# One handover of a transformer block on one core: the first feed-forward unit moved to other PSUM banks and one place ahead on TensorE

## The reference, cut to what matters

```python
# x: (16, 256, 256), cond_emb: (16, 256, 192), 16 heads of 64, D_FF = 1024, float32
h = _layernorm(x, ln1_g, ln1_b)
x = _attention(h, h, sa_wq, sa_wk, sa_wv, sa_wo, sa_bo) + x
h = _layernorm(x, ln2_g, ln2_b)
x = _attention(h, cond_emb, ca_wq, ca_wk, ca_wv, ca_wo, ca_bo) + x
h = _layernorm(x, ln3_g, ln3_b)
p = h @ ff_w1 + ff_b1
a, gate = (p[..., :D_FF], p[..., D_FF:])
h = a * jax.nn.gelu(gate, approximate=False) @ ff_w2 + ff_b2
return h + x
```

## Time and profile before

| | before |
|---|---|
| three runs, us | 1720.36, 1722.38, 1723.20 (median 1722.38) |
| profiled execution, us | 1720.33, span 1718.5 |
| TensorE busy | 1701.5 us, 99% of the span |
| VectorE, ScalarE, GpSimd busy | 86%, 69%, 63% |
| granted TensorE clock, mean | 0.999 |
| chain that ended last | TensorE 94%, VectorE 2%, others 1% or less each |

### The profile page before, as it was taken

The page is one execution under the profiler, slowest core; times in us unless marked ns, Lnnn a source line. Parts: engine busy times, 40 slices in busy tenths (PEclk is TensorE's granted clock), DMA queues, the critical chain, the costliest instruction groups (busy, mean ns, idle before and its releaser), DMA issues.

```text
span 1718.5 us, 42973 instructions
## 1 busy us (share of the span) xinstructions
PE 1701.5 (99%) x13628; PEld 1663.3 (97%) x13628; DVE 1470.9 (86%) x3188; ACT 1186.7 (69%) x3245; POOL 1082.9 (63%) x1808
## 2 busy tenths in 40 slices
PE   8999999999999999999999999999999998999999
PEld 7999999999999999999999999999999997888888
DVE  7888988988888888899999999999999987666665
ACT  6777777777777777777778878777777775222222
POOL 6877777766666666687778777777777664122211
PEclk9999999999999999999999999999999999999999
DMA  6877777676666566667778877776666662212210
GB/s 193 198 179 180 185 180 178 167 180 170 152 153 157 151 161 159 166 166 187 190 190 193 193 194 178 185 180 168 167 167 168 163 171 56 74 50 63 67 44 25
DMA packets 286641, 263.99 MB, mean 154 GB/s; under 512 B 102224, under 2 KB 246736, under 8 KB 286416
## 3 DMA queue, kind: packets, MB, share of 16 engines
q1 hardware_dynamic: 230992, 246.55, 56.9%
q10 hardware_dynamic: 55424, 14.70, 4.0%
HBM read 70.40 MB, written 24.90 MB: 55 GB/s over the span
## 4 chain that ended last, share of the span: by engine, by line
PE 94%; DVE 2%; ACT 1%; POOL 1%; DMA 1%; issue 1%; SPq 1%; ACTq 0%; POOLq 0%; DVEq 0%
PE QKB L341 19%; PE PVB L400 14%; PE PTB L355 12%; PE WOP L380 10%; PE VB L316 9%; PE S L303 7%; PE S L302 7%; PE S L898 5%; PE PTB L898 5%; PE QKB L914 3%; PE VB L914 3%; ACT PT L507 0%; DVE NM L610 0%; ACT PH L526 0%; DVE PL L592 0%
## 5 line engine op out<-in xcount | busy, mean ns | idle before, releaser
L507 ACT ACTIVATE PT<-S,NM 128x256 f32<-128x256 f32 x1024 | 472.1, 474 | 190.3 <-DVE NM L610 189.9
L592 DVE TENSOR_TENSOR PL<-PTB,PH 128x512 fp32r<-128x512 f32 x512 | 349.9, 684 | 85.9 <-ACT PH L526 79.9
L797 POOL TENSOR_TENSOR ON<-ON,RB 128x256 f32<-128x256 f32 x256 | 188.8, 738 | 283.0 <-DVE ON L624 268.6
L526 ACT ACTIVATE PH<-PTB 128x1024 fp32r<-128x1024 f32 x256 | 263.4, 1029 | 94.7 <-PE PTB L355 91.6
L610 DVE TENSOR_REDUCE NM<-S 128x2 f32<-128x512 f32 x512 | 326.1, 678 | 0.4 <-PE S L290 0.3
L355 PE MATMUL PTB<-IDN,PT 128*128 128x128 f32 x2048 | 267.4, 273 | 5.1 <-DVE PL L592 4.9
L302 PE MATMUL S<-RX 128*128 128x256 f32 x1012 | 253.7, 283 | 0.0
L303 PE MATMUL S<-RX 128*128 128x256 f32 x1012 | 253.7, 283 | 0.0
L355 PEld LDWEIGHTS PTB<-IDN,PT 128*128 128x128 f32 x2048 | 230.0, 140 | 7.0 <-DVE PL L592 6.6
L380 PE MATMUL WOP<-WO,OT 128*128 128x256 f32 x1536 | 226.3, 283 | 2.0 <-POOL OT L802 2.0
L624 DVE TENSOR_TENSOR ON<-PVB,ON 64x256 f32<-64x256 f32 x512 | 213.3, 417 | 3.5
(11 more groups left out here) (136 smaller groups left out, 3141.3 us busy)
## 6 DMA issues: line engine op xcount, KB each, us to landing
RX<-QKS SPq DMA_DIRECT2D x506, 192.0 KB, 2.9
RX<-QKS SPq DMA_DIRECT2D x506, 128.0 KB, 2.8
RB<-denominators SPq DMA_DIRECT2D x512, 64.0 KB, 2.6
out_dram<-XR SPq DMA_DIRECT2D x32, 256.0 KB, 2.7
rows<-XN SPq DMA_DIRECT2D x24, 256.0 KB, 2.5
rows<-HF SPq DMA_DIRECT2D x23, 256.0 KB, 2.5
XR<-in_x_dram SPq DMA_DIRECT2D x16, 256.0 KB, 3.1
denominators<-RDT SPq DMA_DIRECT2D x256, 16.0 KB
```

Source lines behind the costliest of these rows:

```text
L507: last = e.activation(PT[:, c % 2, j * S:(j + 1) * S], S1[:, i, qt * S:(qt + 1) * S], ACT.Exp, bias=NM[:, j:j + 1], accum_out=DEN[:, c % 2 ...
L526: e.activation(PH[:, s % 2, :], PTB[:, :, :].rearrange("p i n -> p (i n)"), ACT.Copy) \
L592: e.tensor_tensor(PL[:, cols], PTB[:, i, :], PH[:, s % 2, cols].bitcast(F32), ALU.subtract).then_inc(a.dve_pl, 1)
```

## The change

In the order of the diff:

- `act_slot`: the eight loads of chunk 0's rows are issued two a slot in slots 248 and 249 instead of one a slot in 248 to 251 (on SyncE the same). `act_ffn_h` runs for one half in slot 252 and for the other in 253, ahead of PH there, instead of both in 254. In slot 254, behind PH, the new `act_ffn_round_h` rounds both.
- `dve_slot`: the second half of PL is made right behind the first from slot 254 on; so slot 255 has no left-over half at its start.
- The rounded rows of chunk 0 (and of all even chunks) go to QKS instead of RX.
- Unit 0's F1 goes to the banks QKB and VB (`gates`); `AG` is swapped, so unit 1 goes to S1 and unit 2 to PTB. Unit 0 waits for the last evacuations of QKB and VB, unit 1 for the last exponentials, unit 2 for the last PL.
- `dve_ffn_turn` runs in slots 250 and 251 instead of 252 and 253. `dve_ffn_split` is gone: in slot 254 VectorE waits for the last odd ring copy and makes only the low parts (`dve_ffn_low`).
- In the hand-written loops the unit now comes first, then the slot, on TensorE, VectorE and ScalarE. GpSimd's order is as it was.

```diff
@@ -513,11 +513,10 @@
             elif sl.has(c + AHEAD) and not -1 <= c < DIRECT - 1:
                 act_copy_qk(e, c + AHEAD)
 
-            if ATT - 8 <= c < ATT - 4:
-                load_ffn_rows(e, 0, 2 * (c - ATT + 8) + 1)
-            if c == ATT - 2:
-                act_ffn_h(e, 0, 0)
-                act_ffn_h(e, 0, 1)
+            if ATT - 8 <= c < ATT - 6:
+                load_ffn_rows(e, 0, 4 * (c - ATT + 8) + 1, 4 * (c - ATT + 8) + 3)
+            if c in (ATT - 4, ATT - 3):
+                act_ffn_h(e, 0, c - ATT + 4)
 
             if sl.has(c - 1):
                 s = c - 1
@@ -525,6 +524,10 @@
                 sl.wait(e, a.pe_pv, s - 1)
                 e.activation(PH[:, s % 2, :], PTB[:, :, :].rearrange("p i n -> p (i n)"), ACT.Copy) \
                     .then_inc(a.act_ph, 1)
+
+            if c == ATT - 2:
+                act_ffn_round_h(e, 0)
+                act_ffn_round_h(e, 1)
 
             if prepares and pair == 1:
                 act_load_rows(e, seq + 1, *(range(2, 4) if seq else range(4)))
@@ -613,7 +616,7 @@
             if 0 < c < DIRECT:
                 dve_split_qk(e, c + 2)
 
-            if sl.has(c - 2):
+            if sl.has(c - 2) and c < ATT - 1:
                 dve_p_low(e, c - 2, 1)
 
             if sl.has(c - 3):
@@ -654,6 +657,8 @@
                 sl.wait(e, a.act_ph, c)
                 sl.wait(e, a.pe_pv, c - 1)
                 dve_p_low(e, c - 1, 0)
+                if c >= ATT - 2:
+                    dve_p_low(e, c - 1, 1)
 
             if pair == 3 and c > PAIRS:
                 n = seq - 1
@@ -834,8 +839,9 @@
 
         fs = FfnStages()
 
-        RXF = RX[:, :, :, :, :].rearrange("p r i u s -> p (r i u s)")
-        FHT = ((RXF[:, 0:KD * CW], RXF[:, KD * CW:2 * KD * CW]), (PH[:, 0, :], PH[:, 1, :]))
+        QKF = QKS[:, :, :, :].rearrange("p r u s -> p (r u s)")
+        FHT = ((QKF[:, 0:KD * CW], QKF[:, KD * CW:2 * KD * CW]), (PH[:, 0, :], PH[:, 1, :]))
+        RINGS = sum(k % 2 for k in range(DIRECT, ATT))
 
         def rounded(chunk, part, k):
 
@@ -845,8 +851,12 @@
             .rearrange("p (r a s) -> p r a s", r=2, a=2)
         FG = PT[:, 0, :].rearrange("p (r s) -> p r s", r=2)
         FV = PT[:, 1, :].rearrange("p (r s) -> p r s", r=2)
-        AG = (S1, PTB)
+        AG = (PTB, S1)
         OB = (QKB, VB)
+
+        def gates(c, g):
+
+            return (QKB, VB)[g][:, :] if c == 0 else AG[c % 2][:, g, :]
 
         ROWS = (XN[:, :], HF[:, :])
         TURNED = (STG[:, 0:CW], STG[:, CW:2 * CW])
@@ -884,8 +894,11 @@
                 sl.wait(e, fs.dve_hf, c - 1)
                 if c == 0:
                     e.wait_ge(s_pw, 2 * QTR * NCH)
+                    e.wait_ge(a.dve_lo, ATT)
+                    e.wait_ge(a.dve_vf, ATT)
+                if c == 1:
                     e.wait_ge(a.act_exp, 2 * ATT)
-                if c == 1:
+                if c == 2:
                     e.wait_ge(a.dve_pl, 2 * ATT)
                 if c == FU - 1:
                     pe_ffn_first(e, chunk, f, 0).then_inc(fs.pe_f1, 1)
@@ -895,7 +908,7 @@
                         n = 0
                         for k in range(KD):
                             for wp, ap in ((0, 0), (0, 1), (1, 0)):
-                                last = e.matmul(AG[c % 2][:, g, :], w1(k, wp, g * FF + f * P),
+                                last = e.matmul(gates(c, g), w1(k, wp, g * FF + f * P),
                                                 rounded(chunk, ap, k), start=n == 0, stop=n == 5)
                                 n += 1
                     last.then_inc(fs.pe_f1, 1)
@@ -940,6 +953,11 @@
             e.activation(ROWS[k], ROWS[k], ACT.Identity, bias=LNG[:, 2, 1, k:k + 1],
                          scale=LNG[:, 2, 0, k:k + 1]).then_inc(fs.act_hf, 1)
 
+        def act_ffn_round_h(e, k):
+
+            e.wait_ge(fs.act_hf, k + 1)
+            e.activation(rounded(0, 0, k), ROWS[k], ACT.Copy).then_inc(fs.s_hh, 1)
+
         def act_ffn(e, sl):
             c = sl.c
             if sl.has(c):
@@ -955,7 +973,7 @@
                     e.activation(FG[:, c % 2, S:CW], last_half(1)[:, S:CW], ACT.Gelu,
                                  bias=B1[:, PAIRS + f:PAIRS + f + 1]).then_inc(fs.act_g, 1)
                 else:
-                    e.activation(FG[:, c % 2, :], AG[c % 2][:, 1, :], ACT.Gelu,
+                    e.activation(FG[:, c % 2, :], gates(c, 1), ACT.Gelu,
                                  bias=B1[:, PAIRS + f:PAIRS + f + 1]).then_inc(fs.act_g, 1)
             if c >= 0 and c % PAIRS == 6 and sl.has(c + PAIRS):
                 for k in range(KD):
@@ -970,15 +988,11 @@
                                    TURNED[h].rearrange("p (b k t i) -> p k t b i", b=4, k=KD, t=TT)[:, k])
             last.then_inc(fs.dve_th, 1)
 
-        def dve_ffn_split(e, sl, chunk):
-            for k in range(KD):
-                sl.wait(e, fs.act_hf, KD * chunk + k + 1)
-                if k == 0:
-                    sl.wait(e, fs.pe_f1, PAIRS * (chunk - 1))
-                e.tensor_copy(rounded(chunk, 0, k), ROWS[k]).then_inc(fs.s_hh, 1)
-                sl.wait(e, fs.s_hh, KD * chunk + k + 1)
-                e.tensor_tensor(rounded(chunk, 1, k), ROWS[k], rounded(chunk, 0, k).bitcast(F32),
-                                ALU.subtract).then_inc(fs.s_ht, 1)
+        def dve_ffn_low(e, k):
+
+            e.wait_ge(fs.s_hh, k + 1)
+            e.tensor_tensor(rounded(0, 1, k), ROWS[k], rounded(0, 0, k).bitcast(F32),
+                            ALU.subtract).then_inc(fs.s_ht, 1)
 
         def pool_ffn_split(e, chunk):
             for k in range(KD):
@@ -1013,7 +1027,7 @@
             elif sl.has(c):
                 r = c % 2
                 sl.wait(e, fs.act_g, c + 1)
-                e.scalar_tensor_tensor(FV[:, r, :], AG[r][:, 0, :], B1[:, f:f + 1], FG[:, r, :],
+                e.scalar_tensor_tensor(FV[:, r, :], gates(c, 0), B1[:, f:f + 1], FG[:, r, :],
                                        ALU.add, ALU.mult).then_inc(fs.dve_hf, 1)
                 sl.wait(e, fs.dve_hf, c + 1)
                 sl.wait(e, fs.pe_f2, c - 1)
@@ -1112,10 +1126,12 @@
                 dve_normalize(e, zero_ffn, fs, 0, ROWS, (0, 1))
             if c == ATT - 10:
                 dve_normalize(e, zero_ffn, fs, 0, ROWS, (2, 3))
-            if ATT - 4 <= c < ATT - 2:
-                dve_ffn_turn(e, 0, c - ATT + 4)
-            if c == ATT - 1:
-                dve_ffn_split(e, zero_ffn, 0)
+            if ATT - 6 <= c < ATT - 4:
+                dve_ffn_turn(e, 0, c - ATT + 6)
+            if c == ATT - 2:
+                e.wait_ge(d_dup[1], 16 * COPIES * RINGS)
+                dve_ffn_low(e, 0)
+                dve_ffn_low(e, 1)
 
         def pool_low(e, *ns):
 
@@ -1292,8 +1308,8 @@
                     store_rows(c // PAIRS + 1)
                 if c in (ATT - 10, ATT - 9):
                     store_ffn_rows(0, c - ATT + 10)
-                if ATT - 8 <= c < ATT - 4:
-                    load_ffn_rows(e, 0, 2 * (c - ATT + 8))
+                if ATT - 8 <= c < ATT - 6:
+                    load_ffn_rows(e, 0, 4 * (c - ATT + 8), 4 * (c - ATT + 8) + 2)
                 if 1 <= c <= ATT:
                     save_den(c - 1)
                 if 0 <= c - 1 + AHEAD < ATT and c - 1 >= -AHEAD:
@@ -1351,8 +1367,8 @@
             act_weights(e, 4, 5)
             run_slots(-AHEAD, ATT + 1, ATT, lambda sl: act_attention_slot(e, sl))
             for j in range(2):
+                act_ffn(e, Slot(j, FU, 2))
                 act_slot(e, Slot(ATT + 1 + j, ATT))
-                act_ffn(e, Slot(j, FU, 2))
             ffn(e, act_ffn, 2)
 
         @block.vector
@@ -1375,8 +1391,8 @@
             dve_weights(e, 5)
             run_slots(-AHEAD, ATT + 1, ATT, lambda sl: dve_attention_slot(e, sl))
             for j in range(3):
+                dve_ffn(e, Slot(j, FU, 2))
                 dve_slot(e, Slot(ATT + 1 + j, ATT))
-                dve_ffn(e, Slot(j, FU, 2))
             e.wait_ge(a.dve_xo, 2 * B)
             ffn(e, dve_ffn, 3)
 
@@ -1390,8 +1406,8 @@
             e.wait_ge(s_ring, 4)
             run_slots(-AHEAD, ATT, ATT, lambda sl: pe_attention_slot(e, sl))
             for j in range(4):
+                pe_ffn(e, Slot(j, FU, 2))
                 pe_slot(e, Slot(ATT + j, ATT))
-                pe_ffn(e, Slot(j, FU, 2))
             ffn(e, pe_ffn, 4)
 
 
```

## The result

| | before | after |
|---|---|---|
| median of 13 runs each, us | 1721.35 (1719.46 to 1723.20) | 1725.75 (1723.35 to 1727.67) |
| ratio, 95% interval | | 1.0026 (1.0018 to 1.0033) |
| profiled execution: its time and span, us | 1720.33, 1718.5 | 1726.59, 1724.8 |

The change makes the kernel 4.4 us slower. To compare executions I measure one stretch on TensorE, from the start of PV(249) (slot 251, up to which the PV products start in the same rhythm before and after) to the start of F1(6) (where the rhythm is the same again), and call it **the handover**. It is 55.27 us before (1415.53 to 1470.80) and 60.49 us after (1416.65 to 1477.14): 5.2 us more.

The account below looks back on a forecast made before the run. TensorE bound nearly everywhere; at the handover, its loop with VectorE. Terms 0.63 + 0.17 - 0.33 + 0.18 - 3.0 + 1.7 + 2.2, about +1.5 us, took the profiled execution to 1721.8; forecast 1723.1, range 1719.2 to 1726.2.

Parts of the forecast that it names:

- the likeliest case: Whole kernel: a measured time within 0.2%, 3.4 us, of no change, chance 0.72; the forecast sum was about +1.5 us.
- the rival of the drain: At the table load before gelu(0): a real drain makes F2(0) 1.4 later; +2.9, about 1724.5 us; chance 0.06.
- the clock: Rival: gaps before PV(253) and F2(0) drop TensorE to 1.2 GHz; two falls, +4.7, about 1726.3 us; chance 0.08.
- the loop of TensorE and VectorE: From slot 253 on: NM, PL, ON, PV, PL hold TensorE; waits to F1(0) about 7.7 us, the most returnable.
- Parts 1 and 2: Slots 250 to 253: earlier loads and turns, +0.63; gain and bias a slot apart ahead of PH, +0.17 and -0.33.
- Part 3: Slots 254 and 255: P low in one turn and only low parts on VectorE put PV(253) later, +0.18 more.
- Part 4: Ahead of slot 256: F1(0) follows PV(253) without a wait, none before WO(252), T(255), PV(254); -3.0 us.
- First late unit: Before F2(0): gelu(0) stands behind PH(255) and the table load, so TensorE waits +1.7 us (1.3 to 2.4).
- Second late unit: Before F2(3): GpSimd's OT, bias adds and 1/sigma hang on the later WO(254); TensorE waits +2.2 us (0 to 2.9).

Follow-up runs that it names:

- e8_turn_early: The kernel before with only the earlier row loads and turns and the gain and bias steps in slots 252 and 253 ahead of PH: 1720.38 us.
- e6_gain_behind: e5 with ScalarE's gain and bias steps of slots 252 and 253 behind PH instead of ahead of it: 1719.23 us.
- e3_low_later: The changed kernel with VectorE's two low parts of chunk 0's rows moved from the end of slot 254 to behind ON(252) in slot 255: 1722.71 us.
- e9_table_early: e6_gain_behind with an unread one-column gelu on ScalarE in slot 256, between ON(253) and PH(255), to load the table early: 1717.99 us.
- e2: The changed kernel with GpSimd's 1/sigma for chunk 1 ahead of its four bias adds for chunk 0: 1722.70 us.
- e4: The changed kernel with the edits of e2 and e3_low_later together: 1720.76 us.
- e5: e4 with GpSimd's 1/sigma of chunk 1 moved once more, to ahead of OT(255), behind the product ON of slot 258: 1719.46 us.
- e1_fill: The changed kernel with unread identity transposes filling TensorE's gaps before PV(253), F2(0) and F2(3), every wait kept: 1722.54 us.
- e7_order_back: The changed kernel with the hand-written loops of TensorE, VectorE and ScalarE back to the slot first, then the unit: 1722.15 us.
- e10_pl_apart: The changed kernel with P low in two turns again, the second half at the start of the next slot: 1725.28 us.

## Why the prediction was right and wrong

The time lies in the range (1725.75 in 1719.2 to 1726.2), but the likeliest case was "within 0.2%, +1.5 us" and the measured is +4.4, just beyond it, where I had put 0.18. That it lies in the range is luck. The range's upper end came from the rival of the drain (1724.5 + 1.5, which is 1726.0, not the 1726.2 that I wrote; the lower end adds up to 1719.4, not 1719.2), and no drain showed. The forecast's own time, 1723.1, with the same 1.5 for the spread of runs would have ended at 1724.6, and the rival that came true, the clock, stood at 1726.3, outside. Point by point:

- **Bound by the loop of TensorE and VectorE; gaps, not busy time**: right. All that the experiments gained came from gaps and from the falls of the clock behind them.
- **Parts 1 and 2**, +0.63, +0.17, -0.33 (in sum +0.63, +0.80, +0.47 at PV(250), (251), (252)): measured +0.53, +0.66, +0.35 in after, and the same in e8_turn_early. ScalarE's steps ahead of PH were named as what ate the gain of the turn's removal; e6_gain_behind shows 1.06 us for it.
- **Part 3**, PV(253) at +0.65: measured 22.80 for 21.75, +1.05. The step that was too short is "the two low parts at 1434.6 and 1435.2", 0.61 each: the first took 1.21, and GpSimd's split of V ran at the same time (1435.50 to 1436.23). That these two stand on the path was in the sum, but as a term of a whole of +0.18 it was not seen as what it is, the largest thing to mend: e3_low_later gains 3 us by moving them, 1.6 of it the fall of the clock.
- **Part 4**, F1(0) behind PV(253) without a wait, and none before WO(252), T(255), PV(254): right.
- **First late unit**, +1.7: measured 1.50 idle, 1.65 by start times (1447.34 + 2.75 to 1451.74). The chain (T(255), PH(255), table load, gelu) is as written; e9_table_early takes the load out of it.
- **Second late unit**, +2.2: measured 2.20 idle, 2.36 by starts. e2, e4 and e5 show its cause; VectorE waited 5.28 for 1/sigma.
- **The clock**: this is what the forecast's sum left out. I had it as a rival at 0.08, two falls, +4.7 in all, priced 1.5 each; measured two falls, 1.6 each (e1_fill), +4.4. Its places were half right: behind the gap before PV(253), as written, but not behind the one before F2(0) (1.50), where the clock stayed at 1.00; the second fall came before F2(3), at the gap of 2.20 that the rival had not counted. The argument against it was that from 1430 to 1450 TensorE had been busy 15.6 of 20 us at 1.00. That stretch was too long a look: its gaps were 1.08, 0.85 and 1.32, each on its own:

```profile
1436.47 0.66 PE L355 MATMUL PTB<-IDN,PT 128*128 128x128 f32 x4 [1.08 <-DVE PL L592]
...
1442.05 0.66 PE L355 MATMUL PTB<-IDN,PT 128*128 128x128 f32 x4 [1.32 <-DVE PL L592]
```

Once TensorE is at work, the longest gap in the trace of before is 1.67, at 20.87, and the 0.66 of the earlier trace rows is the fall behind just that one; all others are of 1.32 or less, with the clock at 1.00 behind them. So the rows gave no ground to hold a fall behind gaps of 2.3 and 2.2 us for so unlikely.

Sum of the handover: 1.5 as forecast, 0.4 for part 3, 3.2 for two falls, 5.1 of 5.2. So the forecast's waits held, and what it had wrong was to put the clock at nothing.

The Trainium skill (ScalarE: Activation LUTs, section What ACT_TABLE_LOAD costs) gives a table load 1.28 us and a drain of about 1.38. In after PH(255) ends 1447.60, the load runs 1447.62 to 1448.90 and gelu(0) starts at 1448.91. The load's length agrees; with 0.02 ahead of it and 0.01 behind it the trace has no drain, and the rival that rested on it falls.

## What to carry to other kernels

When a unit is pulled ahead to fill a gap, follow what its own consumers stand behind on each engine: here the gelu behind PH and a table load, and a normalising step behind GpSimd's adds, so that two gaps closed and two opened. Price a TensorE gap that is longer than any that the trace shows at full clock at its length and a fall of the clock behind it (here 1.6 us). Steps that need not be early (low parts, gain and bias, 1/sigma against bias adds) go behind those that the next product waits for: these moves, an early table load and one slot taken ahead of F2(0) turned +4.4 us into -4.6. Which part of the 4.6 needs unit 0's new place is not shown: the same moves with the slot first, as in e7_order_back, were not tried.

## What the runs showed of the hardware

- Behind the gap of 2.46 us (after, e2_rstd_first, e7_order_back) and that of 2.20 (after, e3_low_later, e10_pl_apart) the granted clock fell to 0.50, every time, 0.2 to 1.6 us after TensorE had resumed; behind gaps of 1.78, 1.50 and 1.03 at the handover it did not. Transposes in the gaps held it at 1.00. A shorter gap can go either way from one execution to the next: near the start every kernel has the same gap of 1.67 or 1.68 us, and the clock fell behind it in seven of the thirteen profiled executions (before, e2_rstd_first, e6_gain_behind to e10_pl_apart) and not in the other six. Against the 0.66 of the earlier trace rows the same 4 us of after have

```profile
20.00:24.00 4.00, 2.97 (x28) 2.65 (x29) 3.28 (x7) 3.63 (x14) 3.73 (x7) 1.00 0.03 4
```

- VectorE's steps between SBUF tiles were slow where GpSimd worked: 1.21 for 0.68 (low part beside the split of V), 1.49 and 1.58 for 0.73 (normalising beside bias adds), and GpSimd was slow in turn: 2.98 for 2.82 for its adds, 1.25 for 0.74 for the step on ON beside the low part in e3_low_later. This was seen in four places, not tried on its own.
- A table load was hidden wholly by one gelu of a single column, 0.20 us long, in a wait of ScalarE: load at 1438.90, gelu(0) right behind PH(255) at 1444.00 (e9_table_early).
